# Attention over 64 tokens in fp32: the values' product in 64x64 array tiles, one head and one sequence each

## What is computed

```python
q, k, v = split_heads(x @ W_query), split_heads(x @ W_key), split_heads(x @ W_value)   # 4 heads x 32
scores = einsum('hbqd,hbkd->hbqk', q, k)
out = einsum('hbqk,hbkd->hbqd', softmax(scores, axis=-1), v)       # heads side by side: 128 columns
return relu(out + x @ W_res)
```

## Time and profile before

| | |
|---|---|
| median of 3 runs | 1503.88 us (1503.87 to 1504.69) |
| the profiled execution's own time | 1503.88 us |
| its span in the trace | 1502.1 us |
| PE busy | 1483.0 us (99%) |
| PEld busy | 1340.6 us (89%) |
| DVE busy | 1390.9 us (93%) |
| ACT busy | 1045.8 us (70%) |
| POOL busy | 871.2 us (58%) |
| DMA engines, mean busy share | 4 tenths, 90 GB/s |
| granted PE clock | full from 18 us on (9 tenths or more in all slices) |

### The profile page before, as it was taken

One profiled execution on the slowest core, in us unless ns is written; L12 is line 12 of the kernel. 1 busy time (PEld: TensorE's weight loads), 2 busy tenths in 40 slices (PEclk: granted clock), 3 DMA queues, 4 the chain that ended last, 5 costly groups with the idle time before them and its releaser, 6 DMA issues.

```text
span 1502.1 us, 73982 instructions
## 1 busy us (share of the span) xinstructions
PE 1483.0 (99%) x31232; PEld 1340.6 (89%) x31232; DVE 1390.9 (93%) x1793; ACT 1045.8 (70%) x1794; POOL 871.2 (58%) x1548
## 2 busy tenths in 40 slices
PE   7999999999999999999999999999999999999997
PEld 5999999999999999999999999999999999999996
DVE  6999999999999999999999999999999999999996
ACT  4677777777777777777777777777777777777775
POOL 3655555555555555555555555555555555555555
PEclk9999999999999999999999999999999999999999
DMA  3444444444444444444444444444444444444442
GB/s 58 99 85 97 86 97 86 97 86 96 86 97 86 97 86 96 86 96 86 97 86 96 86 96 86 96 87 96 87 96 86 96 87 96 87 95 87 95 87 76
DMA packets 677301, 135.35 MB, mean 90 GB/s; under 512 B 545888, under 2 KB 677216, under 8 KB 677216
## 3 DMA queue, kind: packets, MB, share of 16 engines
q1 hardware_dynamic: 675840, 134.30, 43.1%
q10 hardware_dynamic: 1376, 0.26, 0.1%
HBM read 67.37 MB, written 67.11 MB: 90 GB/s over the span
## 4 chain that ended last, share of the span: by engine, by line
PE 98%; issue 0%; POOL 0%; DVE 0%; ACTq 0%; ACT 0%; DMA 0%; POOLq 0%
PE ps_so L238 18%; PE ps_pt L229 17%; PE ps_so L217 14%; PE ps_vr L206 8%; PE ps_qk L193 8%; PE ps_qk L195 8%; PE ps_vr L208 8%; PE ps_qk L194 8%; PE ps_vr L207 8%; POOL y L154 0%; DMA w_raw<-in_L_rec_W_res_dram 0%; ACTq L327 0%; POOL v_diag L167 0%; ACT qk L284 0%; DVE row_max L357 0%
## 5 line engine op out<-in xcount | busy, mean ns | idle before, releaser
L154 POOL TENSOR_TENSOR y<-attn,vr 128x256 f32<-128x256 f32 x512 | 386.1, 775 | 523.8 <-DVE attn L372 500.2
L167 POOL COPY v_diag<-vr 64x264 f32<-64x264 f32 x1024 | 478.9, 468 | 102.9 <-POOL y L154 39.9
L304 ACT ACTIVATE probs_t<-ps_pt 128x512 f32<-128x512 f32 x512 | 307.4, 600 | 172.1 <-PE ps_pt L229 172.1
L357 DVE TENSOR_REDUCE row_max<-ps_so 128x16 f32<-128x1024 f32 x256 | 313.5, 1225 | 59.8 <-PE ps_so L217 59.5
L291 ACT COPY vr<-ps_vr 128x512 f32<-128x512 f32 x512 | 300.2, 586 | 62.0 <-PE ps_vr L208 1.4
L284 ACT COPY qk<-ps_qk 128x512 f32<-128x512 f32 x512 | 301.5, 589 | 48.8 <-PE ps_qk L195 9.2
L229 PE MATMUL ps_pt<-ident,shifted 128*128 128x128 f32 x2048 | 321.4, 279 | 0.8 <-ACT probs_t L304 0.8
L362 DVE TENSOR_TENSOR shifted<-ps_so,row_max 128x1024 f32<-128x1024 f32 x256 | 313.5, 1225 | 8.8
L238 PE MATMUL ps_so<-v_diag,probs_t 128*64 128x66 f32 x8192 | 296.1, 224 | 1.5 <-ACT probs_t L304 0.9
L238 PEld LDWEIGHTS ps_so<-v_diag,probs_t 128*64 128x64 f32 x8192 | 260.6, 137 | 36.4 <-issue 1.8
L206 PE MATMUL ps_vr<-w_hi,x_hi 128*128 128x256 f32 x1024 | 288.9, 282 | 0.0
(11 more groups left out here) (20 smaller groups left out, 1235.2 us busy)
## 6 DMA issues: line engine op xcount, KB each, us to landing
x_in<-in_r_x_dram SPq DMA_DIRECT2D x1024, 64.0 KB, 2.2
out_dram<-y SPq DMA_DIRECT2D x256, 256.0 KB, 2.5
w_raw<-in_L_rec_W_query_dram ACTq DMA_DIRECT2D x1, 64.0 KB, 2.2
w_raw<-in_L_rec_W_key_dram ACTq DMA_DIRECT2D x1, 64.0 KB, 2.6
w_raw<-in_L_rec_W_value_dram ACTq DMA_DIRECT2D x2, 32.0 KB, 2.6
w_raw<-in_L_rec_W_res_dram ACTq DMA_DIRECT2D x2, 32.0 KB, 2.5
```

What stands on the lines that cost most here:

```text
L154: nc.gpsimd.tensor_tensor(y[:, n % 2, a * HALF:(a + 1) * HALF].rearrange("k t (p j d) -> k j (t p) d", j=2, d=D), attn[:, n % 2, a * HALF: ...
L167: nc.gpsimd.tensor_copy(v_diag[n % 2][j * F:(j + 1) * F, seq, :, :, :, j].rearrange("k a t p d -> k a (t p) d"), vr[n][seq * F:(seq + 1) * ...
L357: nc.vector.reduce_max(row_max[:, :].rearrange("q (h u) -> q h u", h=HEADS), scores, AX_X).then_inc(max_ready, 1)
```

## The change

The values' product is made in 64x64 array tiles: for each pair, half and tile of tokens, and for each sequence s and each head j of the pair, one matmul with 64 partitions (keys), 64 stationary columns (queries of sequence s) and 33 moving columns. That is 32 matmuls for a group instead of 16. Where s equals j, the moving operand is `vr` itself, since its keys lie on the right partitions; for s other than j it is `v_cross`, which POOL fills with 2 copies for each group instead of 4. `v_diag`, its zeros and its semaphore go. Head j writes to banks 2j and 2j+1, so results are ordered by head, and `inv_sum`, `attn` and the views of them follow; shapes of the DVE and POOL operations keep their element counts. ACT waits for `o_done` of the group four back before it writes `vr` again. PE's four waits ahead of `weigh_values` move into a function `wait_for_values`, which is called for step i+1 ahead of the last matmul of `project_vr(i, n, 1)`, and there in the order shifted_ready, attn_ready, v_moved, pt_ready.

```diff
-        v_diag = [sb(f"v_diag{n}", [P, SEQS, 2, HALF, PAIRS, 2, VW]) for n in range(2)]
+        v_cross = [sb(f"v_cross{n}", [P, 2, HALF, PAIRS, VW]) for n in range(2)]
-        inv_sum = sb("inv_sum", [P, TILES, HEADS])
-        attn = sb("attn", [P, 2, TILES, HEADS, D])
+        inv_sum = sb("inv_sum", [P, HEADS, TILES])
+        attn = sb("attn", [P, 2, 2, TILES, PAIRS, D])
...
                     for j in range(2):
-                        for m, seq in enumerate((1 - j, j)):
-                            nc.gpsimd.tensor_copy(
-                                v_diag[n % 2][j * F:(j + 1) * F, seq, :, :, :, j].rearrange("k a t p d -> k a (t p) d"),
-                                vr[n][seq * F:(seq + 1) * F, :, j].rearrange("k a t p d -> k a (t p) d"),
-                            ).then_inc(v_moved, 1)
-                            if m == 0 or j == 1:
-                                pool.wait_ge(v_moved, i * 4 + j * 2 + m + 1)
+                        nc.gpsimd.tensor_copy(
+                            v_cross[n % 2][j * F:(j + 1) * F].rearrange("k a t p d -> k a (t p) d"),
+                            vr[n][(1 - j) * F:(2 - j) * F, :, j].rearrange("k a t p d -> k a (t p) d"),
+                        ).then_inc(v_moved, 1)
+                        pool.wait_ge(v_moved, halves(i, j))
...
+            def wait_for_values(i):
+
+                if has(i - 1):
+                    pe.wait_ge(shifted_ready, i)
+                if has(i - 3):
+                    pe.wait_ge(attn_ready, i - 2)
+                if has(i - 2):
+                    pe.wait_ge(v_moved, halves(i - 2, 1))
+                    pe.wait_ge(pt_ready, halves(i - 2, 1))
...
                     nc.tensor.matmul(ps, x_hi[n][:, tok], w_vr_lo, start=False, stop=False)
+                    if (a, t) == (1, HALF - 1):
+                        wait_for_values(i + 1)
                     last = nc.tensor.matmul(ps, x_lo[n][:, tok], w_vr_hi, start=False, stop=True)
...
                             for s in range(SEQS):
-                                at = (a * HALF + t) * BANK + O_AT + p * 2 * VW
-                                last = nc.tensor.matmul(
-                                    ps_so[s * F:(s + 1) * F, at:at + 2 * VW],
-                                    probs_t[:, a, t * PAIRS + p, s * F:(s + 1) * F],
-                                    v_diag[n % 2][:, s, a, t, p].rearrange("k j d -> k (j d)"), start=True, stop=True)
+                                for j in range(2):
+                                    at = (j * 2 + a) * BANK + O_AT + (t * PAIRS + p) * VW
+                                    rows, queries = slice(j * F, (j + 1) * F), slice(s * F, (s + 1) * F)
+                                    if s == j:
+                                        values = vr[(n + 2) % RING][rows, a, j, t, p]
+                                    else:
+                                        values = v_cross[n % 2][rows, a, t, p]
+                                    last = nc.tensor.matmul(ps_so[queries, at:at + VW],
+                                                            probs_t[rows, a, t * PAIRS + p, queries], values,
+                                                            start=True, stop=True)
...
             def step(i, n):
-                if has(i - 1):
-                    pe.wait_ge(shifted_ready, i)
-                elif not has(i):
-                    pe.wait_ge(shifted_ready, N)
-                if has(i - 3):
-                    pe.wait_ge(attn_ready, i - 2)
+                if not has(i - 1):
+                    wait_for_values(i)
                 if has(i - 2):
-                    pe.wait_ge(pt_ready, halves(i - 2, 1))
-                    pe.wait_ge(v_moved, (i - 2) * 4 + 4)
                     weigh_values(i - 2, n)
```

More of the change, by code:

```diff
@@ L82, in attention_program @@
         ident_zero, ident_ready = sem("ident_zero"), sem("ident_ready")
-        ones_ready, diag_zero = sem("ones_ready"), sem("diag_zero")
+        ones_ready = sem("ones_ready")
         whi_ready, wlo_ready = sem("whi_ready"), sem("wlo_ready")
@@ L155, in step @@
                             y[:, n % 2, a * HALF:(a + 1) * HALF].rearrange("k t (p j d) -> k j (t p) d", j=2, d=D),
-                            attn[:, n % 2, a * HALF:(a + 1) * HALF].rearrange("k t (p j) d -> k j (t p) d", j=2),
+                            attn[:, n % 2, :, a * HALF:(a + 1) * HALF].rearrange("k j t p d -> k j (t p) d"),
                             vr[(n + 2) % RING][:, a, 2:4, :, :, 0:D].rearrange("k j t p d -> k j (t p) d"),
@@ L177, in _ @@
             last.then_inc(ones_ready, 1)
[L178 to L181, removed]
             pool.wait_ge(ident_zero, 1)
@@ L288, in copy_vr @@
                 if has(i - 4):
-                    act.wait_ge(v_moved, (i - 4) * 4 + 4)
+                    act.wait_ge(v_moved, halves(i - 4, 1))
+                    act.wait_ge(o_done, i - 3)
                     act.wait_ge(sum_ready, halves(i - 4, a))
@@ L353, in step @@
                 scores = bank[:, :, 0:O_AT].rearrange("q h (u f) -> q h u f", f=F)
-                heads = bank[:, :, O_AT:O_AT + HEADS * VW].rearrange("q u (h d) -> q u h d", d=VW)
+                heads = bank[:, :, O_AT:O_AT + HEADS * VW].rearrange("q b (m d) -> q b m d", d=VW)
                 if has(i):
@@ L372, in step @@
                     nc.vector.tensor_tensor(
-                        attn[:, n % 2], heads[:, :, :, 0:D],
-                        inv_sum[:, :, :].unsqueeze(3).to_broadcast([P, TILES, HEADS, D]),
+                        attn[:, n % 2].rearrange("q j (a t) p d -> q (j a) (t p) d", a=2), heads[:, :, :, 0:D],
+                        inv_sum[:, :, :].unsqueeze(3).to_broadcast([P, HEADS, TILES, D]),
                         ALU.mult).then_inc(attn_ready, 1)
```

## The result

| | before | after |
|---|---|---|
| median | 1504.17 us (4 runs) | 1533.09 us (4 runs, 1532.6 to 1533.64) |
| ratio | | 1.0192, 95% interval 1.0174 to 1.021 |
| span of the profiled execution | 1502.1 us | 1531.8 us |

The change makes the kernel 1.9% slower, 29 us or 0.11 us for each of 256 groups. I had forecast 1560 us, 56 us more than before, in a range of 1495 to 1582. The narrower range that I gave for the forecast's own mechanism, 1535 to 1582, lies just above what was measured.

A forecast was written before the change was run, and what follows sets the result against it. PE was taken to bound the step; 0.16 + 0.025 + 0.045 + 0.01 - 0.02 = +0.22 us per step, times 256 groups, +56 us on 1503.88, gave 1560 us, 3.7% slower. Range 1495 to 1582.

The forecast's parts named there:

- PE bounds the kernel, the pauses are the array running empty, the old waits are free: PE sets the 5.77 us step; 0.21 us before weigh is the array emptying; waits end with some 0.15 us to spare.
- A pass is bound by its load: Weigh block: loading 64 stationary columns takes 0.055 of a pass's 0.058 us, so fewer moving columns don't shorten it.
- The two rivals in which the stream matters: Weigh block: passes shrink with moving columns, 1450 us, chance 0.08; or load and stream add up, about 1500, chance 0.09.
- The block changes by -0.02 us.: Weigh block: last stream at most 0.03 us shorter, two more tiles each start 0.007 us later; net -0.02 us.
- +0.01 for the score block.: Score block behind weigh: its instructions may be queued later behind twice as many weigh instructions, +0.01 us, bounds 0 and +0.05.
- The moved waits, +0.16 us in each group.: Last L208 matmul now waits for attn: weigh starts 0.52 us after attn's end instead of 0.36.
- The group with three operations, +0.1 on top.: One group in four has two more sequencer operations behind the attn wait: 0.1 us there, 0.025 on average.
- The branch, +0.18 once in four.: At the loop's end the branch falls between L208 and weigh: weigh at 0.70 us instead of 0.52, 0.045 on average.
- It closes to a loop.: Row maximum to attn, weigh and next row maximum sum to the 5.77 us step, so added waits lengthen each step.
- The rival of covered waits: L208's load can start by 0.04 us after attn, so only -0.02 us a step remains: 1498 or so, chance 0.13.
- The signs of being wrong.: Weigh block clearly under 1 us, L208's last load less than 0.1 us after attn, or DVE's idle time not growing.
- two rivals that did not come true: Waits stay covered, 1498 or so, chance 0.13; load and stream add up, about 1500, chance 0.09.

The follow-up runs named there:

- e2_only_waits_moved: The kernel before with nothing but its waits moved ahead of the last L208 matmul, in the changed kernel's order: 1584.72 us, ratio 1.0533.

## Why the prediction was right, and where its sizes were off

- *PE bounds the kernel, the pauses are the array running empty, the old waits are free*. Right: with the waits back, weigh starts 0.363 us after attn in every group, although the sequencer's operations differ there too.
- *A pass is bound by its load*. Right, and shown both ways: 17 moving columns leave the distance of the passes as it is, 32 stationary ones nearly halve it. The two rivals in which the stream matters fell with that; both expected 0.1 us or more from the narrower stream. Between a tile's first two loads lie 0.055 us with 64 columns and 0.028 with 32.
The Trainium skill's rule for a load's time ("TensorE: Matmul & The Clock Gate", section "LDWEIGHTS (loading the stationary operand)"), columns divided by 1.2 in ns, gives 53 and 27 ns as estimates; the traces agree within 2 ns.
- *The block changes by -0.02 us.* Right, and by both of its parts: from the last load's start to the score's first load it is 0.177 us instead of 0.208, and the last load starts 0.010 later. Together that is -0.021 in three kinds of group. In the group behind the branch it is +0.007: there the loads of three of the four tiles start 0.036 us and more behind the first one's instead of 0.007 and more, and stay that much behind.
- *+0.01 for the score block.* Wrong: from its first to its last matmul it takes 0.70 us before and after.
- *The moved waits, +0.16 us in each group.* Right in kind, wrong in size; this is the step that failed. The term was "L208's load starts 0.11 + 0.09 = 0.20 us after attn". Measured: 0.07 in three groups of four. I had taken the 0.09 from one wait to the next out of the group at the loop's top, where each wait has an operation of its own, and the 0.11 from PE's first load of all. In three groups of four of the kernel after two waits share an operation, and the sequencer is already in it. From load to weigh I had 0.32, and 0.315 was measured in the groups without the branch, but its two parts were right only in sum: L215's matmul starts 0.03 to 0.10 us after its load and not 0.11, and weigh 0.22 to 0.28 after that and not 0.21. So the term is +0.026 us, not +0.16, in the two plain groups.
- *The group with three operations, +0.1 on top.* It is there, once in four, but what it adds over the plain ones is 0.24: 0.31 against 0.07. Mean 0.06 instead of 0.025.
- *The branch, +0.18 once in four.* Measured +0.155 over the plain groups, and the block 0.03 longer. Near.
- *It closes to a loop.* Right: every 0.01 us at weigh is in the step. 0.124 - 0.014 = 0.110 a step, and 0.109 measured. In e2_only_waits_moved +0.323 at weigh and +0.007 in the block stand beside +0.326 measured for the step.
- *The rival of covered waits* was nearer the truth than I gave it. In half the groups only 0.03 us are missing. Its point from which it decides, a load 0.04 us after attn, is where it stands without the moved waits (0.03 to 0.04); 0.07 is just beyond.
- *The signs of being wrong.* I had written that I'd be wrong if L208's last load started less than 0.1 us after attn. In three groups of four it does, at 0.07 us. The loss is there all the same, since in the two plain groups 0.025 us, behind the branch 0.18 and in the group with three operations 0.27 are added at weigh. So that sign was met and the other two, a block clearly under 1 us and no growth of DVE's idle time, were not.

The sum was +0.22 us and the truth +0.11. The path was right, the size is half of what I gave; that 1533 us lies inside my range is owed to its lower end, which I had drawn down for two rivals that did not come true, and not to the forecast's own 1535 to 1582. What was forecast as a gap on PE before L208 is there in 63 groups only; DVE's idle time before the row maximum, forecast to grow by 0.22 us (from 0.21 to 0.43), grew by 0.12 on average.

What stays open: why the same four waits get one packing in one kernel and another in the next. The runs show the packings and their prices, not the rule. That a change of the waits' target values from multiples of four to multiples of two brings it about was only thought of, not tried.

The best of these kernels that computes everything is e1_waits_back, the new tiles with the old place of the waits: 1502.08 us, 0.15% under the kernel before (0.9985, 0.9976 to 0.9994), a gain at the edge of what can be told.

## What to carry to other kernels

Ask of a small fp32 matmul which of load and stream is longer before narrowing one of them; where they are equal, halving the moving side gives only the end of the last stream. A wait that is satisfied late belongs where the array must pause anyway: moved ahead of one more matmul, it puts that matmul, its load and the pause behind it on the loop. Its price is what the queue's sequencer does between the signal and the next instruction, and that must be read in each step of the loop, not in one.

## Not expected of the hardware

- A sequencer operation behind a late wait costs 0.10 us on PE. The next load starts 0.07 us after the DVE operation ends if that wait is the second of two in an operation in which the sequencer already stands, 0.116 us if it is the first or the only one, and 0.31 to 0.33 us after it with three operations.
- PE's loop over 8 groups instead of 4 made the kernel 23% slower than the kernel after (1883.7 against 1533.1 us), with 349 instruction packets instead of 14.
- Every kernel of this study with 64x64 tiles and PE's loop over 4 groups has one or two steps of 7.2 to 7.7 us once, between 32 and 48 us, instead of 5.5 to 5.9, and no kernel with 128x64 tiles has one over 6.4. That the longer program of PE (14 instruction packets against 11) is the cause wasn't tried.
- An fp32 matmul's moving column costs 0.8 ns in each of its two passes (13 ns for 16 columns), and a stationary column about as much (a load occupies its tile for 0.055 us with 64 columns, 0.028 with 32).
